# Two transformer layers on one core: a routed stage in another order, and one value product moved one program earlier

## What is computed

```python
x = LN(x + latent_attention(x))   # 32 heads, causal, q/k through low-rank latents
x = LN(x + routed_lora(x))        # x W^T + b + (masked x A^T) B^T, rank picked per token
x = LN(x + alibi_attention(x))    # 32 heads of 16, q/k layer-normed, v clipped, causal
x = LN(x + gated_ffn(x))          # silu(g) * u, 1792 wide
```

## Time and profile before

| | us |
|---|---|
| runs, median of 3 | 1521.06 |
| lowest and highest run | 1517.84, 1523.41 |
| the profiled execution | 1517.3 |
| its span | 1515.1 |
| PE busy | 1431.2 (94%) |
| DVE busy | 889.8 (59%) |
| ACT busy | 812.1 (54%) |
| POOL busy | 534.1 (35%) |

### The profile page before, as it was taken

One profiled execution on the slowest core, in us unless ns is written; L12 is line 12 of the kernel. 1 busy time (PEld: TensorE's weight loads), 2 busy tenths in 40 slices (PEclk: granted clock), 3 DMA queues, 4 the chain that ended last, 5 costly groups with the idle time before them and its releaser, 6 DMA issues. The chain is left out here.

```text
span 1515.1 us, 23953 instructions
## 1 busy us (share of the span) xinstructions
PE 1431.2 (94%) x8208; PEld 1010.9 (67%) x8208; DVE 889.8 (59%) x1361; ACT 812.1 (54%) x1731; POOL 534.1 (35%) x495
## 2 busy tenths in 40 slices
PE   5799999999999999999978987999999999999996
PEld 4566776776777676677646864555555568888885
DVE  4345554555554445555567636766666427767867
ACT  3556765666666565676534322555565665332433
POOL 0234444433445433444033134404131014444442
PEclk9799999999999999999989998999999999999998
DMA  5243334333324323333410045433435033000000
GB/s 188 69 50 44 40 50 53 34 49 39 42 47 53 38 46 48 42 39 41 88 56 1 1 56 71 68 47 58 56 51 103 40 114 123 1 1 1 1 28 28
DMA packets 61664, 75.89 MB, mean 50 GB/s; under 512 B 20640, under 2 KB 42144, under 8 KB 60704
## 3 DMA queue, kind: packets, MB, share of 16 engines
q1 hardware_dynamic: 57248, 64.55, 24.6%
q0 software_dynamic: 4352, 10.49, 5.0%
HBM read 42.49 MB, written 2.10 MB: 29 GB/s over the span
## 5 line engine op out<-in xcount | busy, mean ns | idle before, releaser
L738 DVE TENSOR_REDUCE nmax<-sc 128x1 f32<-128x128 f32 (+7 forms) x256 | 193.0, 754 | 181.1 <-PE sc L485 180.4
L1630 ACT ACTIVATE l_probs<-l_banks 128x512 f32<-128x512 f32 (+3 forms) x366 | 165.8, 495 | 134.1 <-PE l_banks L1574 82.9
L1670 DVE TENSOR_REDUCE pm<-l_sm 128x2 f32<-128x1024 f32 (+1 forms) x192 | 178.5, 956 | 97.3 <-PE l_sm L1544 61.5
L666 ACT COPY pt<-tb 128x512 f32<-128x512 f32 (+3 forms) x256 | 129.4, 505 | 194.8 <-PE tb L499 191.8
L658 ACT ACTIVATE probs<-sc,nmax 128x128 f32<-128x128 f32 (+7 forms) x256 | 190.4, 744 | 31.8 <-DVE nmax L738 28.4
L499 PE MATMUL tb<-ident,probs 128*128 128x128 f32 x1152 | 173.4, 276 | 1.8 <-ACT pt L666 1.1
L78 PE MATMUL sc<-k_h,q_h 128*128 128x512 f32 (+4 forms) x384 | 144.4, 376 | 8.1 <-DVE q_l L762 7.4
L1571 PE MATMUL l_banks<-qk_bufs 128*128 128x512 f32 (+3 forms) x366 | 135.1, 411 | 0.8 <-ACT l_probs L1630 0.4
L521 PE MATMUL mb<-pt,ckv 128*64 128x512 f32 (+2 forms) x736 | 131.7, 493 | 2.1 <-DVE x_tok L732 0.2
L78 PE MATMUL sc<-k_l,q_h 128*128 128x512 f32 (+4 forms) x384 | 132.1, 344 | 0.0
L78 PE MATMUL sc<-k_h,q_l 128*128 128x512 f32 (+4 forms) x384 | 131.5, 342 | 0.0
(11 more groups left out here) (287 smaller groups left out, 3089.7 us busy)
## 6 DMA issues: line engine op xcount, KB each, us to landing
gated_late<-in_gated SPq DMA_DIRECT2D x11, 768.0 KB, 14.4
wout<-in_w_out SPq DMA_DIRECT2D x16, 512.0 KB, 4.5
late<-late SPq DMA_DIRECT2D x128, 64.0 KB, 2.0
rb<-rT SPq DMA_DIRECT2D x248, 32.0 KB, 4.5
qk_bufs<-late SPq DMA_DIRECT2D x96, 64.0 KB, 5.9
qk_bufs<-late POOLq DMA_DIRECT2D x96, 64.0 KB, 7.0
nope_t<-in_nope_by_dim SPq DMA_DIRECT2D x16, 192.0 KB, 3.9
late<-in_gated SPq DMA_DIRECT2D x3, 768.0 KB, 7.9
```

The lines of the kernel that those rows point to most:

```text
L666: act.copy(pt[i // 4][:, e, j0:j0 + nb, (i % 4) * P:(i % 4 + 1) * P], tb[TB[g]][:, 0:nb, :]).then_inc(pt_act, 1)
L738: dve.tensor_reduce(nmax[:, n % 4:n % 4 + 1], row, axes, ALU.max, negate=True).then_inc(negmax, 1)
L1630: act.activation(probs[(NC * g + c) % RING][:, h, 0:w], e_slot(g, n)[:, 0:w], ACT.Exp).then_inc(exped, 1)
L1670: dve.tensor_reduce(pm[g % 2][:, :, s, i, half], slot(("m", g, n))[:, :, 0:w], AX.X, ALU.max, negate=True).then_inc(freed, 1)
```

## The change

It moves steps, and moves one of the eight value products.

- In the tail of the first attention, tiles 4 to 7 get no statistics; DVE makes them in the routed stage, after it has lowered tiles 0 to 3.
- In the routed stage PE turns tiles 4 to 7 together behind `base(0)` and `back(0)`, does `back(1)` before `turn_lo(0)` and `base(4)` before `turn_lo(1)`. ACT's copies of weights, its roots and `normalise(0)` stand in another order. The eight bias additions go from POOL to DVE, in four places.
- The value product of tile 7 is made behind the last projection and copied to keep.v by DVE.
- In the second attention V_TILES = 7 value products remain. All of tile 5 and half of tile 6 stand before the first maxima unit, the other half beside the first two units; units 2 to 7 stand alone.
- POOL clears and loads set 1, waits for `rows_first`, and only then moves the keys of group 1; set 2 follows.

```diff
@@ stage_mla, DVE
                     dve.tensor_tensor(keep.x[:, j, :], tail_bank(j), keep.x[:, j, :], ALU.add).then_inc(tail_read, 1)
-                    dve.wait_ge(tail_read, j + 1)
-                    keep.n1.stats(dve, j, keep.x[:, j, :])
+                    if j < 4:
+                        dve.wait_ge(tail_read, j + 1)
+                        keep.n1.stats(dve, j, keep.x[:, j, :])
@@ stage_front, PE
+                def project_v(j):
+                    pe.wait_ge(wqh, 3 * DK)
+                    pe.wait_ge(wql, 3 * DK)
+                    pe.wait_ge(clip, len(order) - 3)
+                    first, rest = split_terms(cols(j), wqkv_h[2], wqkv_l[2])
+                    three(pe, po[0][:], first + rest).then_inc(qkv_ps, 1)
...
                 down_rank(0)
-                turn_x1(4)
-                turn_x1(5)
                 base(0)
                 back(0)
-                turn_x1(6)
-                turn_x1(7)
+                for j in range(4, ST):
+                    turn_x1(j)
                 base(1)
                 down_rank(1)
                 base(2)
+                back(1)
                 turn_lo(0)
-                back(1)
                 base(3)
-                turn_lo(1)
                 for j in range(4):
                     lora(j)
                 for j in range(4, ST):
                     base(j)
+                    if j == 4:
+                        turn_lo(1)
                     lora(j)
...
+                project_v(ST - 1)
@@ stage_front, ACT
                 upper_x(0, 0)
-                n1.root(act, 4, ST, 1)
                 upper_x(1, 1)
...
                 w_copy(2)
                 w_copy(3)
+                act.copy(b_hh[:], bT2).then_inc(w_h, 1)
+                n1.root(act, 4, ST, 1)
+                qkv_copy(0, range(2))
                 act.wait_ge(n1.inv_ok, 4)
...
-                act.copy(b_hh[:], bT2).then_inc(w_h, 1)
                 ag_copy(0)
+                qkv_copy(0, range(2, DK))
                 for j in range(4, ST):
                     upper_x(j, j)
-                qkv_copy(0, range(DK))
-                qkv_copy(1, range(2))
+                qkv_copy(1, range(DK))
                 ag_copy(1)
                 upper_lo(0)
-                qkv_copy(1, range(2, DK))
+                n2.root(act, 0, 1, 0)
+                n2.root(act, 1, 2, 1)
+                normalise(0)
                 upper_lo(1)
@@ stage_front, DVE
+                def add_bias(j):
+                    dve.wait_ge(tr_ps, j + 1)
+                    dve.tensor_tensor(keep.x[:, j, :], keep.x[:, j, :], bias, ALU.add).then_inc(biased, 1)
...
+                for j in range(4):
+                    lower_x(j, j)
+                for j in range(4, ST):
+                    n1.stats(dve, j, keep.x[:, j, :])
                 n1.variance(dve, 4, ST)
                 n1.inverse(dve, 4, ST, 1)
                 dve.wait_ge(n1.inv_ok, 3)
                 n1.normalise(dve, 4, keep.x[:, 4, :])
                 n1.normalise(dve, 5, keep.x[:, 5, :])
-                for j in range(3, ST):
+                dve.wait_ge(keep.small_in, 16)
+                for j in range(2):
+                    add_bias(j)
+                for j in range(4, ST):
                     lower_x(j, j)
                 route(0)
+                for j in range(2, 4):
+                    add_bias(j)
                 lower_lo(0)
                 route(1)
+                add(0)
+                add(1)
+                n2.inverse(dve, 0, 1, 0)
                 lower_lo(1)
...
                 n2.inverse(dve, 3, 4, 3)
+                for j in range(4, ST):
+                    add_bias(j)
                 for j, ready in ((4, (0, 1)), (5, (2, 3)), (6, (4,)), (7, (5,))):
                     add(j)
...
+                dve.wait_ge(qkv_ps, len(order) + 1)
+                dve.tensor_copy(keep.v[:, ST - 1, :], po[0][:])
@@ stage_front, POOL
-                for j in range(ST):
-                    pool.wait_ge(tr_ps, j + 1)
-                    pool.tensor_tensor(keep.x[:, j, :], keep.x[:, j, :], bias, ALU.add).then_inc(biased, 1)
@@ stage_alibi: V_TILES = ST - 1 replaces ST in the waits on vp (SP) and v_ev (PE, POOL)
-    order = [...] + [("v", k, j) for j in range(6) for k in range(DK)]
-    late_v = [("v", k, j) for j in (6, 7) for k in range(DK)]
+    order = [...] + [("v", k, j) for j in range(V_TILES - 1) for k in range(DK)]
+    late_v = [("v", k, V_TILES - 1) for k in range(DK)]
+    order += late_v[0:2]
     for n in range(M_HALF):
-        order += [("m", 0, n), late_v[n]]
+        order += [("m", 0, n)] + late_v[2 + n:3 + n]
@@ stage_alibi, POOL
-                for b in range(1, BUFS):
-                    pads(b)
-                    load_rows(b)
-                    if b == 1:
-                        move_keys(1)
-                        values(1, 1)
-                        pool.wait_ge(vx_ok, 2)
+                pads(1)
+                load_rows(1)
+                pool.wait_ge(rows_first, ROWS)
+                move_keys(1)
+                values(1, 1)
+                pool.wait_ge(vx_ok, 2)
+                pads(2)
+                load_rows(2)
```

More of the change, by code:

```diff
@@ L1130, in _ @@
                     act.activation(x, x, ACT.Identity, bias=n1.shift[:, j:j + 1], scale=n1.inv[:, 0, j:j + 1]).then_inc(x_late, 1)
-                act.copy(b_hh[:], bT2).then_inc(w_h, 1)
                 ag_copy(0)
+                qkv_copy(0, range(2, DK))
                 for j in range(4, ST):
                     upper_x(j, j)
-                qkv_copy(0, range(DK))
-                qkv_copy(1, range(2))
+                qkv_copy(1, range(DK))
                 ag_copy(1)
                 upper_lo(0)
-                qkv_copy(1, range(2, DK))
+                n2.root(act, 0, 1, 0)
+                n2.root(act, 1, 2, 1)
+                normalise(0)
                 upper_lo(1)
-                n2.root(act, 0, 1, 0)
-                for j in range(1, 4):
+                for j in range(2, 4):
                     n2.root(act, j, j + 1, j)
@@ L1212, in clipped @@
                     nqk.stats(dve, n, dest[c][:, j, :])
+                for j in range(4):
+                    lower_x(j, j)
+                for j in range(4, ST):
+                    n1.stats(dve, j, keep.x[:, j, :])
                 n1.variance(dve, 4, ST)
-                lower_x(0, 0)
                 n1.inverse(dve, 4, ST, 1)
                 dve.wait_ge(n1.inv_ok, 3)
-                lower_x(1, 1)
                 n1.normalise(dve, 4, keep.x[:, 4, :])
-                lower_x(2, 2)
                 n1.normalise(dve, 5, keep.x[:, 5, :])
-                for j in range(3, ST):
+                dve.wait_ge(keep.small_in, 16)
+                for j in range(2):
+                    add_bias(j)
+                for j in range(4, ST):
                     lower_x(j, j)
-                dve.wait_ge(keep.small_in, 16)
                 route(0)
+                for j in range(2, 4):
+                    add_bias(j)
                 lower_lo(0)
                 route(1)
+                add(0)
+                add(1)
+                n2.inverse(dve, 0, 1, 0)
                 lower_lo(1)
-                add(0)
-                for j in range(1, 4):
+                for j in range(2, 4):
                     add(j)
@@ L1308 @@
 AHEAD = 4
+V_TILES = ST - 1
 def chunk_cols(c):
@@ L1329, in alibi_order @@
 def alibi_order():
-    order = [("build", 0, 0), ("build", 0, 1), ("cast", 0, 0), ("cast", 0, 1)] + [("v", k, j) for j in range(6) for k in range(DK)]
-    late_v = [("v", k, j) for j in (6, 7) for k in range(DK)]
+    order = [("build", 0, 0), ("build", 0, 1), ("cast", 0, 0), ("cast", 0, 1)] + [("v", k, j) for j in range(V_TILES - 1) for k in range(DK)]
+    late_v = [("v", k, V_TILES - 1) for k in range(DK)]
+    order += late_v[0:2]
     for n in range(M_HALF):
-        order += [("m", 0, n), late_v[n]]
+        order += [("m", 0, n)] + late_v[2 + n:3 + n]
     order += [("top", 0, 0), ("m", 0, M_HALF), ("rows", 0, 0)]
@@ L1483, in _ @@
                 maxima(0, 0)
-                sp.wait_ge(vp, ST)
+                sp.wait_ge(vp, V_TILES)
                 move(sp, 1, 0, moved)
@@ L1560, in e @@
                         pe.wait_ge(rows_first, ROWS)
-                        pe.wait_ge(v_ev, ST)
+                        pe.wait_ge(v_ev, V_TILES)
                     if n == (0 if g else HG * C_HALF):
@@ L1757, in _ @@
                     pool.wait_ge(ones, PADS[0] + 2 * u + 2)
-                pool.wait_ge(v_ev, ST)
+                pool.wait_ge(v_ev, V_TILES)
                 values(0, 0)
                 pool.wait_ge(vx_ok, 1)
-                for b in range(1, BUFS):
-                    pads(b)
-                    load_rows(b)
-                    if b == 1:
-                        move_keys(1)
-                        values(1, 1)
-                        pool.wait_ge(vx_ok, 2)
+                pads(1)
[6 more added lines that the diff above has]
+                load_rows(2)
```

## The result

Six runs of the changed kernel have a median of 1509.91 us (1507.2 to 1513.45), six of the kernel before 1519.45 us (1516.84 to 1523.41). The ratio is 0.9941, with a 95% interval of 0.9928 to 0.9954: 9.0 us less, where 1512.0 with a gain of 9.0 was forecast. A second series on another occasion gave 0.9930 (0.9914 to 0.9946).

The account below looks back on a forecast made before the run. PE's waits at two barriers (4.5, 4.4 us) and for query and key moves (6.8) were the bound. Routed stage -1.5, builds -0.55, units -1.85, landing -4.1, clock -1.0 sum to -9.0: 1512 from the median; range 1505 to 1520.

Parts of the forecast that it names:

- Barrier one and the first part: Tail to base(1): statistics leave the tail, first turn 3.45 us earlier, down_rank(0) 4.9, base(1) 2.0 with blocked DVE adds.
- The clock: Routed stage, first part: PE stays at 2.4 GHz because the gap at the first barrier is now 1.1 us.
- Middle: Routed stage, base(1) to turn_x2(2): about 29.0 us against 28.84; the 3.07 us wait returns as 1.8, 2.0 and 3.6.
- The late spell: From turn_x2(2): new idle of 3.6 us may drop PE to half speed, losing about 1.7 us.
- Value product: Second barrier: tile 7's product fills 2.8 of PE's 4.4 us idle at no cost; the half-speed spell behind it goes.
- The units: Second attention, first 8 maxima units: 7.6 us instead of 9.45, a gain of 1.85 us.
- The landing: Second attention, group 1's moves: land at 927.2 to 930.5, so m(1,0) starts 8.0 us earlier, 4.1 of it the wait.
- rival A: Chance 0.25: maxima DMAs meet row loads, POOL's wait delays keys, PE idles about 5 us at m(1,0); about -3.5 us, 1517.5.
- The clock term: Second attention behind m(1,0): idle shrinks below 1 us, the half-clock spell until about 947 vanishes, giving about 1.0 us.
- POOL's added wait: Second attention: waiting for rows_first holds group 1's keys some 4 us, mostly hidden by SP's transfers; unhidden, 4.94 us returns.
- rival B: Chance 0.17: POOL and DVE miss each other, no blocks, clock stays up; routed stage -3.8, in all -12, 1509.
- C: Chance 0.10: DVE bounds the routed stage, every two-SBUF-input instruction blocked; about +4 us, 1525.

Follow-up runs that it names:

- x3: Changed kernel with DVE's bias adds moved into its gaps and POOL's load_rows(1) behind the wait for rows_first; 0.9933 of the kernel before.
- e1: Kernel before with only the value product of tile 7 moved, POOL's old loop kept, so keys don't wait for rows_first; 0.9998 of the kernel before.
- e7: Kernel before with the value product moved and POOL's new order and wait, routed stage and bias adds as before; 0.9963 of the kernel before.
- e3: Changed kernel with POOL's old loop, group 1's keys moved without waiting for rows_first; 0.9978 of the kernel before.
- e8: Kernel before with all eight value products ahead of the first maxima unit, none moved, plus POOL's new order and wait; 0.9982 of the kernel before.
- x1: Changed kernel with DVE's bias adds elsewhere: six behind route(0), two behind n2.inverse(0); 0.9924 of the kernel before.
- e5: Kernel before with only the statistics of tiles 4 to 7 deferred to the start of the routed stage; 0.9997 of the kernel before.
- e2: Kernel before with deferred statistics, new routed order and bias adds on DVE, value products and POOL's loop as before; 0.9964 of the kernel before.

## Why the prediction was right

**Barrier one and the first part.** Right to 0.05 us at the first turn and at down_rank(0). At base(1) it was 0.9 us too careful: DVE came to the normalises 0.2 us sooner than forecast, the two took 1.98 where 2.3 was forecast, and the two adds 3.45 where 3.7 was. All four or nearly all were blocked, as forecast (0.48 and 0.6 each when POOL is idle). The clock was wrong: I took 2.4 GHz, as the gap was 1.1 us, but it fell all the same. The granted clock after (columns as in the earlier trace rows):

```profile
784.00:786.00 2.00, 2.00 (x6) 1.15 (x5) 1.93 (x5) 0.00 (x0) 2.00 (x3) 0.50 0.40 148
...
824.00:826.00 2.00, 2.00 (x8) 1.81 (x8) 1.66 (x5) 1.01 (x3) 0.00 (x0) 0.50 0.00 0
...
884.00:886.00 2.00, 2.00 (x11) 1.66 (x10) 2.00 (x3) 1.11 (x2) 1.82 (x1) 1.00 0.00 0
...
934.00:936.00 2.00, 1.77 (x6) 0.68 (x4) 2.00 (x2) 0.00 (x0) 0.00 (x0) 0.50 0.03 6
```

PE had been busy about half of the time since the barrier, in pieces between DVE's waits, so a short barrier gap did not save it. In nine of the ten profiles with that gap (1.05 us) it fell in this part; in x3's it stayed at full speed. The spell was 3.5 us long, not 10, and lay on down_rank(0).

**Middle.** base(1) to turn_x2(2) took 28.69 us, forecast 29.0, before 28.84; the three waits that replace the old one of 3.07 were 1.6, 1.8 and 3.3 (forecast 1.8, 2.0 and 3.6); at the last two PE had waited 1.27 and 0.95 before as well. The late spell came where it was feared and cost 1.5 us between turn_x2(2) and the first projection (9.77 instead of 8.28; forecast 1.7). In the second profile it came earlier and cost nothing there, and barrier two is 3.0 us earlier instead of 1.6. So the match with the forecast's -1.5 at barrier two is luck with that spell.

**Value product.** Hidden, as forecast: PE's idle at barrier two is 1.7 instead of 4.4 and the barrier waits for ACT as before. The spell behind it went (row at 884): all four profiles of kernels without the product there have it, none of the ten with it.

**Second attention.** The units gave 1.73 (forecast 1.85). The landing gave the most, as forecast: m(1,0) -8.45 (forecast -8.0), -6.47 in the second profile. Two terms offset one another: the moves of group 0 landed 1 us sooner than I had it, and the maxima DMAs took 1.47 longer, which I had only in rival A. The clock term, m(1,0) to the second chunk's build, was -1.5 in the first profile and -0.6 in the second (forecast -1.0), although the spell that I said would vanish came, shorter (row at 934).

**The step that was wrong though the sum was right** is the one on POOL's added wait: "it holds the keys by some 4 us, which SP's transfers in the same full DMA mostly hide". That delay was hidden, as m(1,0) shows no DMA wait, but the step left out what the wait is for. By e1 against e7 it is the whole gain of the value move, and by e3 more than half of the gain of the change. In the sum I had treated the four small DMAs as free of the traffic around them. Without the wait they are not (10.05 us to e(0,0)), and the -3.9 at e(0,0) would have been +0.9. That the sum held is owed to a line of the diff whose use I had not seen.

**The match itself.** The gain of the runs is 9.0 us in the first series and 10.6 in the second, so the size is right; the single terms are not confirmed to tenths. Two traces of the same kernel give -10.0 and -7.1 at the second chunk's build, where the sum had -9.0. In rival B the printed -12 should be -11.3 by its own terms.

**Rivals.** A was wrong (no wait at m(1,0)), though the maxima DMAs did meet the row loads, as it said; B is refuted (adds were blocked, clock fell), and C, that DVE bounds the stage, is half true: DVE sets the pace from turn_lo(0) to turn_x2(2), at no loss against before. The forecast that the blocks would cost what the rule says held. The Trainium skill (SBUF — State Buffer, "Who interferes with whom") has a VectorE instruction with two SBUF inputs contend with a GpSimd instruction that reads SBUF, and the one that comes second fully blocked. By the adds at 1.7 us against 0.6 the trace agrees.

## What to carry to other kernels

Before filling an engine's idle earlier, look at which transfers it releases and what small, urgent DMAs they will meet: here 0.77 MB of keys issued beside 16 KB of maxima made PE wait 5.8 us for the maxima, 1.3 with the keys held back, and that one semaphore wait won 5 to 7 us of the time. Buffers that lie over the operands of a late product tie two unrelated things together, so finishing that product sooner can pay even where its own time is not saved (e8, 2.7 us). And put VectorE's work with two SBUF inputs where VectorE would idle and GpSimd does not run: in x1 the adds took 0.6 us each and barrier two came 1.9 us earlier.

## What the runs showed of the hardware

A block of DVE by POOL isn't bounded by one instruction. In e7's profile, with the routed stage in the old order, the tiny comparison took 8.98 us (8.93 in e8's), against 0.18 in the earlier trace rows, 0.24 in e1's and 0.67 in e5's (timeline of DVE of e7):

```profile
797.79 8.98 DVE L1191 TENSOR_TENSOR less<-gate,top 128x16 f32<-128x16 f32 x1
```

POOL ran without a pause until 806.73, and the comparison ended 0.04 us later (timeline of POOL of e7):

```profile
789.20 10.10 POOL L1272 TENSOR_TENSOR x_tok<-x_tok,late 128x512 f32<-128x512 f32 x8
799.22 5.08 POOL L1275 TENSOR_TENSOR qk_bufs<-late,qk_bufs 128x512 fp32r<-128x512 f32 x4
804.23 2.50 POOL L1275 TENSOR_TENSOR wk_l<-l_q,qk_bufs 128x512 fp32r<-128x512 f32 x2
```

The next base product started 5 us late by it (37.5 instead of 32.6 us from the tail), and barrier two 3.6. POOL's run ended there only because it waited for ACT, which stood behind the same comparison. So of five profiles with the old order of the routed stage two have the long block; the nine with the new order all have 0.7 to 0.9 us at this comparison and 2.5 at the products behind it. Whether the long block differs from execution to execution or from kernel to kernel is open, as only one execution of each was traced. The spread of the runs does not tell: 9.7 us over e7's twelve, but 6.9 over e8's twelve and 6.9 over 23 of the kernel before.

It is likely that many untraced runs of the old order have it: the traced executions of e1 and e5, with short blocks, were the fastest of their eleven runs (4.2 and 4.8 us under the median), while e7's and e8's, with the long one, were 1.6 and 0.2 us under their medians. That would explain why e2 gained more in the runs (5.5) than in its trace (3.7), and that a part of the new order's gain is to avoid the long block, which the prediction did not have. It is not shown.
